# A graph network on one core: column look-ups of the later score stages as four matmuls of 32 weight columns in place of two of 64

## What is computed

```
f1 = relu(x[row] @ nb_W[l] + nb_b[l]);  f2 = relu(x[col] @ self_W[l] + self_b[l])
h = relu(concat([f1, f2]) @ att1_W[l] + att1_b[l])
mask = clip(sigmoid(h @ att2_W[l] + att2_b[l]) * (ZETA - GAMMA) + GAMMA, 0, 1)
rowsum = segment_sum(mask, row) + 1e-6;  d = clip(rowsum ** -0.5, 0, 10)
x = segment_sum((mask * d[row] * d[col])[:, None] * x[col], row);  out = out + x
```

## Time and profile before

| what | value |
| --- | --- |
| median of 3 runs | 9017.37 us (9011.83 to 9018.22) |
| span of the profiled execution | 9016.0 us |
| TensorE matmul busy | 7666.3 us (85%), 306604 matmuls |
| VectorE busy | 7826.6 us (87%) |
| ScalarE, GpSimd busy | 3219.1 us, 3583.6 us |
| score stages of layers 2 and 3 | about 3750 to 4866 us and 5883 to 6995 us of the span |
| mean granted TensorE clock | 0.936 of full speed |

### The profile page before, as it was taken

How to read it: one execution, slowest core, us unless ns; L and a number is a source line. 1 busy time by engine, 2 the same in 40 slices (tenths; PEclk the granted TensorE clock), 3 DMA queues, 4 the chain that set the end, 5 groups by cost and what they waited for, 6 DMA issues and landing times. The chain is left out here.

```text
span 9016.0 us, 756759 instructions
## 1 busy us (share of the span) xinstructions
PE 7666.3 (85%) x306604; PEld 7395.1 (82%) x306604; DVE 7826.6 (87%) x13976; ACT 3219.1 (36%) x6511; POOL 3583.6 (40%) x4126
## 2 busy tenths in 40 slices
PE   0011489999998999899998999999999999969998
PEld 0011378888888999799998999889998999969997
DVE  9999889999998888788888888788887888888887
ACT  0010257777774444300002444410000444434442
POOL 0000500000006888300003888610000788868885
PEclk9855699999998999999999999999999999989997
DMA  1000267778775666577776666577777666646663
GB/s 31 0 0 0 74 230 259 258 260 260 258 254 162 178 178 179 148 227 226 225 227 184 178 177 178 146 207 226 225 227 208 174 178 178 178 131 178 178 177 106
DMA packets 981451, 1593.43 MB, mean 177 GB/s; under 512 B 248148, under 2 KB 729902, under 8 KB 980976
## 3 DMA queue, kind: packets, MB, share of 16 engines
q1 hardware_dynamic: 955338, 1563.58, 58.7%
q0 software_dynamic: 26016, 28.56, 1.8%
HBM read 1308.70 MB, written 283.01 MB: 177 GB/s over the span
## 5 line engine op out<-in xcount | busy, mean ns | idle before, releaser
L1170 PE MATMUL bank<-tab,extra 128*64 128x64 bf16 x201684 | 3512.8, 197 | 214.4 <-DVE tab L1551 118.4
L1170 PEld LDWEIGHTS bank<-tab,extra 128*64 128x64 fp8e4 x201684 | 3430.0, 112 | 284.3 <-issue 256.0
L777 POOL TENSOR_TENSOR planes<-planes 128x448 f32<-128x448 f32 (+1 forms) x2744 | 2596.2, 949 | 503.9 <-DVE planes L1959 439.3
L1003 ACT CAST bank<-planes 128x448 f32<-128x448 bf16 (+1 forms) x2744 | 1471.4, 545 | 1679.3 <-DVE planes L1952 1679.3
L1959 DVE TENSOR_TENSOR planes<-planes,bank 128x448 f32<-128x448 f32 (+1 forms) x2744 | 1709.8, 623 | 224.8 <-ACT bank L1003 208.6
L1952 DVE TENSOR_TENSOR planes<-bank,mask_all 128x448 f32<-128x448 f32 (+2 forms) x2744 | 1666.3, 619 | 242.1 <-PE bank L1170 158.8
L1297 PE MATMUL bank<-planes,extra 128*64 128x192 bf16 x39200 | 1843.3, 248 | 22.5 <-POOL planes L777 10.0
L1297 PEld LDWEIGHTS bank<-planes,extra 128*64 128x64 fp8e4 x39200 | 1688.9, 108 | 66.5 <-issue 16.5
L708 POOL DMA_INDIRECT xg<-q_table,ixb x294 | 277.3, 943 | 3452.1 <-DVE extra L1831 3120.2
L1831 DVE SCALAR_TENSOR_TENSOR extra<-bank,a2w 128x448 f32<-128x448 f32 (+1 forms) x2058 | 1263.7, 629 | 253.9 <-PE bank L1193 211.8
L1193 PE MATMUL bank<-plb,extra 128*128 128x64 bf16 x44100 | 1467.7, 194 | 9.4 <-issue 6.5
(11 more groups left out here) (261 smaller groups left out, 4298.8 us busy)
## 6 DMA issues: line engine op xcount, KB each, us to landing
extra<-one_hots SPq DMA_DIRECT2D x1372, 352.0 KB, 3.1
extra<-one_hots SPq DMA_DIRECT2D x2156, 224.0 KB, 4.0
extra<-one_hots SPq DMA_DIRECT2D x588, 208.0 KB
one_hots<-extra SPq DMA_DIRECT2D x490, 224.0 KB, 4.8
one_hots<-extra SPq DMA_DIRECT2D x294, 352.0 KB, 4.0
work<-slot_rows_cols SPq DMA_DIRECT2D x196, 352.0 KB, 4.9
work<-slot_rows_cols SPq DMA_DIRECT2D x294, 224.0 KB, 5.0
work<-slot_rows_cols SPq DMA_DIRECT2D x98, 208.0 KB
```

Of the source, the lines that this page charges most:

```text
L777: nc.gpsimd.tensor_tensor(tiles(yrl[:, 2, a * C:b * C]), tiles(yrl[:, 1, a * C:b * C]), upper[:, 1, a:b, :], ALU.subtract).then_inc(low_re ...
L1003: nc.scalar.copy(tiles(z_banks[g][:, 0:(b - a) * C]), upper[:, 0, a:b, :]).then_inc(high_ps, 1)
L1170: mm = pe.matmul(bank[half * S:(half + 1) * S, i * C:(i + 1) * C], oct_[:, k * P + half * S:k * P + (half + 1) * S], tab[:, at:at + C], st ...
```

## The change

`cols` gets a parameter `parts`. With two it does what it did. With four, a group and plane takes four matmuls of 32 weight columns and 64 moving columns, to the PSUM partitions 0, 32, 64 and 96 onwards; the first two read the table slice of block 2k, the last two that of block 2k+1. `cols_of` asks for four in the score stages of layers 2 and 3, and for two in the first; segment stages keep two. Results go to the same places of the same banks.

```diff
-            def cols(t, g, first=False):
+            def cols(t, g, first=False, parts=2):
...
                     for pl in range(NPL):
-                        for half in range(2):
-                            at = (pl * NB + 2 * k + half) * C
-                            mm = pe.matmul(bank[half * S:(half + 1) * S, i * C:(i + 1) * C],
-                                           oct_[:, k * P + half * S:k * P + (half + 1) * S], tab[:, at:at + C],
-                                           start=(i == 0 and pl == 0), stop=True, skip_group_check=True)
+                        for part in range(parts):
+                            a, b = part * P // parts, (part + 1) * P // parts
+                            at = (pl * NB + 2 * k + a // S) * C
+                            mm = pe.matmul(bank[a:b, i * C:(i + 1) * C], oct_[:, k * P + a:k * P + b], tab[:, at:at + C],
+                                           start=(i == 0 and pl == 0), stop=True, skip_group_check=True,
+                                           tile_position=(0, a) if parts == 4 else None)
...
                 def cols_of(t, g):
-                    mm = cols(t, g, first)
+                    mm = cols(t, g, first, 2 if first else 4)
```

## The result

The changed kernel takes 11492.02 us, median of 4 runs (11430.78 to 11579.44), against 9017.8 for the kernel before: a ratio of 1.2753, 95% interval 1.2713 to 1.2793. That is 2474 us more, outside the range of 9000 to 10600 us. The profiled execution has a span of 11577.7 us.

A forecast was written before the change was run, and what follows sets the result against it. The prediction took TensorE's pace to bound the two later score stages. Pace 159, sequencer 29 and first-loaded code 15 gave 203 us on a span of 9016.0, with the median 1.4 above it: 9220 us, range 9000 to 10600 us.

The forecast's parts named there:

- What bounds the stages: Later score stages run at TensorE's pace; d us a tile in `cols` moves the end by 196 d.
- first rival: TensorE's loop code in the later score stages no longer fits and is fetched again; two forms, chances 0.18 and 0.12.
- 37.5 ns a set, no misses: The forecast for `cols`: four matmuls take 37.5 ns against 32.0, no code fetched again; 9220 us, chance 0.46.
- One miss a pass: Loop of the later score stages: each way back misses once, 655 us to double, 9875 to 10530 us; chance 0.18.
- the blocks in turn: Loop's 8 code blocks push each other out, 30.7 us a tile, +3600 us, about 12800 us; chance 0.12.
- The forecast's own range: Whole kernel: 9130 to 9330 us, from sequencer at 0 to 40 ns a set with more waits uncovered.
- Pace of a set: `cols`: streaming 26.7 ns plus 2.7 for each of four matmuls, 0.81 us a tile, 159 us in all.
- Sequencer: `cols`: waits and steps less covered by issued matmuls, 0.15 us a tile, 29 us; upper bound 0.77 us.
- a cost of each place: `cols`: 5.3 ns for a matmul on part of the array, set stays 32.0 ns, 9060 us; chance 0.06.
- the faster one: `cols`: loads of 32 weight columns finish in time, set takes 29.1 ns, 8977 us; chance 0.07.
- floor for each matmul: `cols`: 16.0 ns least for a matmul with its load, set takes 64 ns, 9980 us; chance 0.09.
- code is fetched for the first time: First tile and first loop pass of the changed stages: 4.6 more blocks of 256 instructions, taken as 15 us.

The follow-up runs named there:

- the run with its code moved: The changed kernel with 100 small matmuls (200 instructions) ahead of everything on TensorE, in idle time: 9326.35 us, ratio 1.0346.
- the run with 244 ahead: The changed kernel with 122 small matmuls (244 instructions) ahead on TensorE, leaving 4 instructions in the last of the loop's 8 blocks: 9327.5 us.
- the run with the waits in front: The changed kernel with the later score stages' waits for a tile's look-ups moved ahead of its first matmul: 9897.93 us, ratio 1.0980.
- the pace runs: Two runs of the kernel before with loops of 96 equal matmuls (one, two or four sharing the array) in idle time; paces read, no total given.
- first pace run: The kernel before with added loops of equal matmuls at 64, 4, 192 and 128 moving columns; four take 7.9 ns a matmul at 4 columns.

## Why the prediction was wrong

- **What bounds the stages**: right. 1.44 us more a tile on TensorE without refetch, times 196, are 282 of the 312 us of the run with its code moved.
- **The failed step is the choice between the forecast and its first rival.** The prediction gave 0.46 to "37.5 ns a set, no misses" and 0.30 to a loop that no longer fits. The rival's working held: 1608 instructions, an edge at 56, 8 blocks. The trace of before couldn't show the room, and the forecast took the side on which it suffices. Measured: a loop of 7 blocks stays, with the one behind it; of 8 it doesn't, once more than a few instructions lie in the last. That is the room of 8 blocks, 2048 instructions, which the Trainium skill ("Runtime: NRT & Kernel Launch", Instruction fetch mechanics) states; these runs agree with that figure, and not with the two blocks that the same section names further down as the whole room. It should have moved the chance. That 8 blocks stay when the last holds only 4 instructions only the run with 244 ahead shows.
- **The rival's price**: mis-sized in both forms, and the result fell between them. "One miss a pass" gave at most 10530 us, "the blocks in turn" 12800. From one branch back to the next, a pass that fetches takes 33.1 us in the mean of 108, near the 30.7 of the second form, and one that doesn't 12.47; but only 108 of 192 ways back lead to one that does. 108 x 20.6 us are 2227 of the 2256 us by which the profiled executions differ (11577.7 and 9321.5 us). Each packet is late for the next, as the earlier trace rows had it, and the fetching passes also run mostly at half clock, as the stretch of 0.57 shows. Why a pass in between finds all its blocks I can't say. With 9 blocks none does.
- **The range**: 10600 left the blocks in turn out at 0.12. The forecast's own range has an error beside: with the sequencer at 0 its terms give 9017 + 159 + 15 = 9191 us, not 9130.
- **Pace of a set**: wrong in its reason. I took 37.5 ns from a cost of 2.7 for each matmul; between the holes it is 4 x 7.87 = 31.5 ns in the run with its code moved, and 32 to 33 in the run with the waits in front, and comes from issue, 7.9 to 8.4 ns there for a load with its matmul. The pair's 32.0 has another cause, so 0.81 us a tile from pace became about nothing. By the 4 ns for each further tile of the Trainium skill ("TensorE: Matmul & The Clock Gate", Part 3, the measured speedup), 40.0 ns as an estimate, it would have been further off. The rival "a cost of each place" had the right size by accident; the faster one had the likely cause for the pair, and issue took the gain away. The "floor for each matmul" existed, at half the size given.
- **Sequencer**: mis-sized, 0.15 us a tile taken, 0.77 as the upper bound, about 1.4 measured. In the run with its code moved the 588 take (6.07 - 0.197) = 5.87 us where 587 x 7.9 ns are 4.64: 1.23 us stand in the six places between parts, and 0.20 more ahead of `rows`. From start to start the steps there are 0.18 us four times and 0.29 twice, ahead of the parts 3 and 5, which wait for one-hots as well; at no other place is a step longer than 0.02 us. The cover that I counted, matmuls issued ahead, isn't there at all when issue sets the pace. The weight loads show the two longer ones:

```profile
4409.87 2.54 PEld L1174 LDWEIGHTS bank<-tab,extra 128*32 128x32 fp8e4 x264 [0.29 <-issue]
4412.58 1.60 PEld L1174 LDWEIGHTS bank<-tab,extra 128*32 128x32 fp8e4 x168 [0.17 <-issue]
4414.35 1.50 PEld L1174 LDWEIGHTS bank<-tab,extra 128*32 128x32 fp8e4 x156 [0.17 <-issue]
4416.13 0.36 PEld L1197 LDWEIGHTS bank<-plb,extra 128*128 128x128 fp8e4 x10 [0.28 <-issue]
```

- **Sum without refetch**: 203 us forecast, 312 measured. The size was near by two errors that partly cancel, 0.81 too much for pace and 1.25 too little for waits. The remaining 30 us lie mostly where code is fetched for the first time: from the last branch of the stage ahead to the first one of the loop, a stretch with the first tile and the first pass, 137.8 and 137.1 us pass in place of 123.2 and 125.1, 26.6 us more, of which 4 x 1.44 are counted already. That leaves 21 us (15 forecast), which I assign to the code without a run that shows it alone.

No version run here beats the kernel before.

## What to carry to other kernels

Before a change that multiplies the instructions of a loop, count them and where the block edges fall, and compare the loop with what stays loaded (here a loop of 7 blocks of 256, with the next); a shift of 8 instructions elsewhere was worth 2.1 ms. Packets of the instruction queue and long loop branches are the first rows to look at when an engine idles for "issue". Splitting pairs that already filled the array gained nothing here, and once issue set the pace, every wait between matmuls became visible.

## What the runs showed of the hardware

- A loop of 1608 instructions ran without refetch in 7 blocks of 256 (69 packets, 9324 to 9326 us) and in 8 with 4 in the last (9327.5 us); in 8 with 12, 16 or 56 in the last it refetched after 98 to 108 of 192 branches back, 9.0 packets each time.
- A pass behind a long branch (4.9 to 6.9 us in the changed kernel) took 33.1 us in place of 12.47.
- Issue of a weight load and its matmul takes 7.9 ns at the least, at 4 moving columns (half clock) as at 64 (full clock), and up to 10.3 in some passes of the pace runs.
- A pair with 64 weight columns each takes 31.8 ns at 64 and at 48 moving columns (full clock) and 53.2 at 4 (half clock).
- The granted clock was at half in the stretches of 4 moving columns of the first pace run, with TensorE never idle, as this stretch of pairs shows, and it came back in the stretch of 192 columns:

```profile
72.00:90.00 18.00, 18.00 (x682) 0.50 0.00 1
110.00:160.00 50.00, 50.00 (x609) 1.00 0.00 0
```

- `scatter` takes 85.5 ns a pair, the pace run 82.5 for the same shape with other operands. The 3 ns that misled the prediction there stay unexplained.
